# The second expert layer in units of 128 slots, its weights split beforehand in the first attention, and its biases added by VectorE

## The reference

```python
x = x + L0_xattn(ctx, layernorm(x))   # 8 heads of 128, 2113 keys for each batch, 512 queries
x = x + L0_ffn(layernorm(x))          # 8 experts, top 2, fixed capacity of 512
x = x + L1_xattn(ctx, layernorm(x))   # 8 heads of 32, the context asks
x = x + L1_ffn(layernorm(x))          # 8 experts, top 2, as below

def L1_ffn(xf):                       # T = 2048 tokens, D = 256, H = 1024, E = 8
    logits = xf @ Wr + br
    masked = where(logits >= second_largest(logits), logits, -inf)
    weights = softmax(masked)
    h = gelu(xf @ W1[e] + b1[e])      # exact gelu, for every expert e
    out = sum_e weights[:, e] * (h @ W2[e] + b2[e])
```

## Time and profile before

| | |
|---|---|
| time, three runs | 2556.87, 2563.03, 2564.49 us; median 2563.03 |
| profiled execution | 2561.1 us, its span 2559.4 us |
| busy share of the span | PE 89%, DVE 75%, ACT 74%, POOL 71% |
| second expert layer | from 2206 to the end of the span |
| mean granted TensorE clock | 0.967 of full speed |

### The profile page before, as it was taken

The page is one execution under the profiler, slowest core; times in us unless marked ns, Lnnn a source line. Parts: engine busy times, 40 slices in busy tenths (PEclk is TensorE's granted clock), DMA queues, the critical chain, the costliest instruction groups (busy, mean ns, idle before and its releaser), DMA issues. The chain is left out here.

```text
span 2559.4 us, 48371 instructions
## 1 busy us (share of the span) xinstructions
PE 2289.2 (89%) x16979; PEld 1395.7 (55%) x16980; DVE 1921.2 (75%) x3499; ACT 1899.9 (74%) x2979; POOL 1818.0 (71%) x1580
## 2 busy tenths in 40 slices
PE   5999999999999999999998589968888888689996
PEld 3454545444454445445554378835555555468775
DVE  7888778887778887878787556558989899666443
ACT  4787887878877878878888556538879789667554
POOL 2687877787777878777778477617878689556653
PEclk9999999999999999999999699989999999679998
DMA  5000000000000000000000375441202020375323
GB/s 151 1 1 1 27 1 1 1 1 1 27 1 1 1 1 1 1 1 1 1 1 1 106 174 146 97 111 32 60 20 61 11 52 2 126 195 127 49 43 64
DMA packets 90974, 108.66 MB, mean 42 GB/s; under 512 B 18866, under 2 KB 80259, under 8 KB 90707
## 3 DMA queue, kind: packets, MB, share of 16 engines
q1 hardware_dynamic: 68500, 80.57, 10.4%
q0 software_dynamic: 21696, 24.98, 6.3%
q10 hardware_dynamic: 544, 0.00, 0.0%
HBM read 68.75 MB, written 25.88 MB: 37 GB/s over the span
## 5 line engine op out<-in xcount | busy, mean ns | idle before, releaser
L432 POOL TENSOR_TENSOR a_acc<-a_acc,a_pf 128x512 f32<-128x512 f32 (+1 forms) x480 | 679.7, 1416 | 279.9 <-ACT a_pf L601 258.2
L906 DVE TENSOR_TENSOR a_pl<-a_pf,a_ph 128x512 f16<-128x512 f32 x448 | 470.7, 1060 | 23.5 <-ACT a_ph L607 23.5
L2218 POOL TENSOR_TENSOR c_pl<-c_pf,c_ph 128x512 f16<-128x512 f32 x320 | 377.0, 1207 | 118.1 <-ACT c_ph L2315 117.7
L601 ACT ACTIVATE a_pf<-a_psS 128x1024 f32<-128x1024 f32 (+1 forms) x288 | 280.8, 975 | 108.7 <-PE a_psS L624 102.5
L882 DVE TENSOR_REDUCE a_mx<-a_psA 128x1 f32<-128x512 f32 x504 | 330.7, 681 | 26.9 <-PE a_psA L681 25.4
L607 ACT ACTIVATE a_ph<-a_psS 128x1024 f16<-128x1024 f32 (+1 forms) x288 | 281.1, 976 | 0.0
L553 ACT ACTIVATE a_psS<-a_mb 128x1024 f32<-128x1024 f32 x255 | 248.7, 975 | 5.0
L1314 DVE TENSOR_TENSOR f_xn<-f_xn 128x256 f16<-128x256 f32 x312 | 129.6, 424 | 153.2 <-ACT f_xn L1283 126.1
L2551 DVE TENSOR_REDUCE c_wf<-c_psA 128x1 f32<-128x512 f32 x384 | 239.7, 679 | 6.3 <-PE c_psA L2387 5.2
L2308 ACT ACTIVATE c_pf<-c_psS 128x1024 f32<-128x1024 f32 x192 | 201.6, 1050 | 50.6 <-PE c_psS L2416 46.0
L1468 POOL DMA_INDIRECT f_sums<-f_xn,f_sidx x78 | 141.6, 1815 | 135.0 <-DVE f_xn L1867 108.4
(11 more groups left out here) (365 smaller groups left out, 6357.2 us busy)
## 6 DMA issues: line engine op xcount, KB each, us to landing
f_stage<-in_L_ffn_w SPq DMA_DIRECT2D x16, 1024.0 KB
f_stage<-in_L_ffn_W SPq DMA_DIRECT2D x16, 1024.0 KB
c_kst<-c_khs SPq DMA_DIRECT2D x64, 100.1 KB, 2.2
a_cx<-in_ctx SPq DMA_DIRECT2D x4, 1536.0 KB
c_cx<-in_ctx SPq DMA_DIRECT2D x12, 512.0 KB, 3.8
f_sums<-X SPq DMA_DIRECT2D x2, 2048.0 KB, 13.4
f_xrow<-f_xn SPq DMA_DIRECT2D x8, 512.0 KB, 4.8
c_kst<-c_kls SPq DMA_DIRECT2D x32, 100.1 KB, 2.2
```

Of the source, the lines that this page charges most:

```text
L432: g.tensor_tensor(acc[0:k, p, :], acc[0:k, p, :], pf[0:k, q % RF, i, :], ALU.add).then_inc(s_acc, 1)
L601: act.activation(pf[0:r, q % RF, 0:k, :], psS[q % 2][0:r, 0:k, :], ACT.Exp, scale=SCALE).then_inc(s_pF, 1)
L906: v.tensor_tensor(pl[0:r, q % RP, i, :], pf[0:r, q % RF, i, :], ph[0:r, q % RP, i, :], ALU.subtract).then_inc(s_pL, 1)
L2218: g.tensor_tensor(pl[0:r, q % RP, i, :], pf[0:r, q % RF, i, :], ph[0:r, q % RP, i, :], ALU.subtract).then_inc(s_pG, 1)
```

## The change

1. **Units.** In the second expert layer each chunk of 256 slots is made of two units of 128 slots, each with an expert of its own. The table has one number for a unit (HI = 40 entries), padding goes to a multiple of 128, and the number of chunks is 20: half of 32 + 7 units, rounded up. `pe_hidden` does 2 units x 2 parts x 3 matmuls of 128 columns; `pe_output` has the same six matmuls of 256 columns, whose weights now come from two experts. `expert_of` and DVE's `chunk_experts` load two numbers a chunk, and b1 and gates are fetched by unit. PE loads the first numbers before its first `pe_turn`.
2. **Weights.** They are split in the first attention, in 32 pieces of 128x1024 weights, four for each expert (`PIECE_AT`): 19 stand behind unit 3 of a head, 13 behind unit 6. SP loads 512 KB into `tmp`, ACT makes the high half (L599) after the `fill` at the end of unit u, DVE the low half (L966) at the end of unit u + 1, and SP stores both to DRAM (`f1_split`). The second expert layer loads 2 MB of split weights for each expert straight into `w16`; the staging and both split operations are gone there.
3. **Biases.** ACT's gelu has no bias; DVE adds b1, scaled by WS, to the PSUM bank (`dve_add`, L1371, 128x256) and ACT waits for that. The addition for f + 1 stands before the low half of f. `take` of chunk n - 1 stands behind the low half of f = 0 of chunk n.

```diff
+    PIECE_AT = [(n, u) for n in range(NH - 1) for u in (3, 6)
+                if (n < NH - H0 and (n % H0 in (0, 6, 7) or (n % H0 == 1 and u == 3)))
+                or (n >= NH - H0 and (u == 3 or n < NH - H0 + 4))]
...
+            def piece(i):
+                e, second, j = piece_of(i)
+                if i:
+                    sp.wait_ge(s_plo, i)
...
+                    sp.dma_start(wpf, io["L1_ffn_W1"][e, j * P:(j + 1) * P, :]).then_inc(s_pld, 16)
+                sp.wait_ge(s_plo, i + 1)
+                sp.dma_start(wsp[e, :, 2 * second:2 * second + 2, j * 1024:(j + 1) * 1024], wps).then_inc(s_wsp, 16)
...
+            def piece_hi(i):
+                act.wait_ge(s_pld, 16 * i + 16)
+                if i:
+                    act.wait_ge(s_wsp, 16 * i)
+                act.activation(wps[:, 0, :], wpf, ACT.Copy, scale=WS).then_inc(s_phi, 1)
...
+            def piece_lo(i):
+                v.wait_ge(s_phi, i + 1)
+                v.scalar_tensor_tensor(wps[:, 1, :], wpf, WS, wps[:, 0, :], ALU.mult, ALU.subtract).then_inc(s_plo, 1)
...
-    NC = E * CAP // CH if layer == 0 else 2 * T // CH + E - 1
+    NC = E * CAP // CH if layer == 0 else -(-(2 * T // P + E - 1) // IT)
...
-            ps = psH[hidden_slot(L, n, f)][:, 0:CH]
-            for k in range(KC):
-                ks = slice(k * F + f * P, k * F + (f + 1) * P)
-                a, b_ = (w16[:, bass.ds(e, 1), part, ks].rearrange("p a f -> p (a f)") for part in (0, 1))
-                pe.matmul(ps, a, xh[:, p, k, :], start=(k == 0), stop=False)
-                pe.matmul(ps, a, xl[:, p, k, :], start=False, stop=False)
-                ins = pe.matmul(ps, b_, xh[:, p, k, :], start=False, stop=(k == KC - 1))
+            wide = CH // len(es)
+            for u, e in enumerate(es):
+                cs = slice(u * wide, (u + 1) * wide)
+                ps = psH[hidden_slot(L, n, f)][:, cs]
+                for k in range(KC):
+                    ks = slice(k * F + f * P, k * F + (f + 1) * P)
+                    a, b_ = (w16[:, bass.ds(e, 1), part, ks].rearrange("p a f -> p (a f)") for part in (0, 1))
+                    pe.matmul(ps, a, xh[:, p, k, cs], start=(k == 0), stop=False)
+                    pe.matmul(ps, a, xl[:, p, k, cs], start=False, stop=False)
+                    ins = pe.matmul(ps, b_, xh[:, p, k, cs], start=False, stop=(k == KC - 1))
...
-            return pe.value_load(table[0:1, n:n + 1], min_val=0, max_val=E - 1)
+            return tuple(pe.value_load(table[0:1, n * IT + u:n * IT + u + 1], min_val=0, max_val=E - 1)
+                         for u in range(IT))
...
-                bs = b1e[:, p, f:f + 1] if layer else 0.0
+                bs = b1e[:, p, 0, f:f + 1] if layer and not added else 0.0
-                act.wait_ge(L.hP, n * FT + f + 1)
+                act.wait_ge(L.hB if added else L.hP, n * FT + f + 1)
...
+        def dve_add(v, L, n, f):
+            ps = psH[hidden_slot(L, n, f)][:, 0:CH].rearrange("p (u t) -> p u t", t=P)
+            v.wait_ge(L.b1, n + 1)
+            v.wait_ge(L.hP, n * FT + f + 1)
+            v.tensor_tensor(ps, ps, b1e[:, n % 2, :, f:f + 1].broadcast_to([P, IT, P]), ALU.add).then_inc(L.hB, 1)
...
+                if added and not (last and f == FT - 1):
+                    dve_add(v, L, n + (f + 1) // FT, (f + 1) % FT)
...
+                if added and f == 0 and n >= 1:
+                    v.wait_ge(L.hU, done(FT, n - 1, FT - 1))
+                    take_before(n - 1)
...
+            def load_split(e):
+                sp.dma_start(w16[:, e, :, :], wsp[e]).then_inc(s_w[e % 2], 16)
```

More of the change, by code:

```diff
@@ L372, in _ @@
                 load_rows(b)
[L373 to L376 removed]
+            def piece(i):
+                e, second, j = piece_of(i)
+                if i:
+                    sp.wait_ge(s_plo, i)
+                sp.wait_ge(s_xl, sum(1 for w in TORD if IDX[w] < IDX[("M", PIECE_AT[i][0] + 1, 0, 0)]))
+                if second:
+                    sp.dma_start(wpf.rearrange("p (f d) -> p f d", d=D),
+                                 io["L1_ffn_W2"][e].rearrange("(f p) d -> p f d", p=P)[:, 4 * j:4 * j + 4, :]
+                                 ).then_inc(s_pld, 16)
+                else:
+                    sp.dma_start(wpf, io["L1_ffn_W1"][e, j * P:(j + 1) * P, :]).then_inc(s_pld, 16)
+                sp.wait_ge(s_plo, i + 1)
+                sp.dma_start(wsp[e, :, 2 * second:2 * second + 2, j * 1024:(j + 1) * 1024], wps).then_inc(s_wsp, 16)
+            context = 1
+            for i, (n, _) in enumerate(PIECE_AT):
+                while context < B and (context - 2) * H0 + H0 - 3 < n:
+                    sp.wait_ge(s_it, IDX[("T", context - 1, 9)] + 1)
+                    load_context(context)
+                    context += 1
+                piece(i)
         @block.gpsimd
@@ L969, in attention0, with experts @@
     return used
-def experts(nc, X, identf, io, layer, yd, out, pool_sems, small, cleared, load_early=None, early_stats=None):
+def experts(nc, X, identf, io, layer, yd, out, pool_sems, small, cleared, load_early=None, early_stats=None, split=None):
     E, F = 8, 1024
@@ L1149, in __init__ @@
                 self.hP = sem(name + "hP")
+                self.hB = sem(name + "hB") if layer and name == "m" else None
                 self.hH = sem(name + "hH")
@@ L1235, in pe_chunk @@
                 pe.wait_ge(L.xL, n + 3)
-            if splits and layer:
-                pe.wait_ge(s_wl, (n + 3) * PIECES)
+            if layer and L is main and not last:
+                pe.wait_ge(s_wl, e_next[-1] + 1)
             elif splits and p == 1:
@@ L1271, in act_chunk @@
             n = m * 2 + p
-            if layer:
+            added = layer and L is main
+            if layer and not added:
                 act.wait_ge(L.b1, n + 1)
@@ L1320, in dve_chunk @@
                     split_low(v, e, q)
-            v.wait_ge(L.hU, done(FT, n, FT - 1))
-            take(n)
-        LOOPS = ((0, (E - 2) // 2, True), ((E - 2) // 2, PAIRS, False)) if layer else ((0, PAIRS, True),)
+            if not added or last:
+                v.wait_ge(L.hU, done(FT, n, FT - 1))
+                take(n)
+        LOOPS = ((0, PAIRS, not layer),)
         TAIL = range(2 * PAIRS, NC)
@@ L1348, in load_weights @@
                 sp.dma_start(dst, src).then_inc(s_w[half], 16)
-            for half in range(2):
-                load_weights(0, half)
+            def load_split(e):
+                sp.dma_start(w16[:, e, :, :], wsp[e]).then_inc(s_w[e % 2], 16)
+            if layer:
+                sp.wait_ge(s_wsp, 16 * 4 * E)
+                load_split(0)
+            else:
+                for half in range(2):
+                    load_weights(0, half)
             sp.dma_start(yd[0:T, :].rearrange("(t p) c -> p t c", p=P), X[:, :, :]).then_inc(s_base, 16)
@@ L1364, in _ @@
                 sp.dma_start(wrow[T:T + CH, :].rearrange("(t p) e -> p t e", p=P), wst[:, 0:IT, :]).then_inc(s_wd, 16)
-            for half in range(2):
-                load_weights(1, half)
-            with sp.Fori(2, E) as e:
+            if layer:
+                load_split(1)
+                for e in range(E):
+                    sp.wait_ge(s_w[e % 2], 16 * (e // 2 + 1))
+                    sp.sem_inc(s_wl, 1)
+                    if e + 2 == E - 1:
+                        sp.wait_ge(s_bst, 16 * NQ)
+                    if e + 2 < E:
+                        load_split(e + 2)
+            else:
                 for half in range(2):
-                    load_weights(e, half)
+                    load_weights(1, half)
+                with sp.Fori(2, E) as e:
+                    for half in range(2):
+                        load_weights(e, half)
             if load_early:
@@ L1551, in _ @@
             act_turn(act, main, 0, 0)
-            if layer:
-                for q in range(PH, PIECES):
-                    split_high(act, 1, q)
             for first_m, last_m, splits in LOOPS:
@@ L1811, in _ @@
                 v.tensor_scalar(wst[:, :, :], sc[:, :, :], 1.0 / WS, None, ALU.mult).then_inc(s_wst, 1)
-            if layer:
-                for q in range(PH):
-                    split_low(v, 0, q)
             v.wait_ge(s_rk, 1)
@@ L1858, in _ @@
                 v.sem_inc(s_tab, 1)
-                for q in range(PH):
-                    split_low(v, 1, q)
             def take_rows(m, p):
```

154 lines of the change are left out of this document (92 added, 62 removed).

## The result

The changed kernel takes 2630.46 us (median of 4 runs, 2629.3 to 2630.88) against 2563.76 us before (4 runs in the same comparison): ratio 1.0267, 95% interval 1.0255 to 1.0279. It is slower by 67 us, outside the predicted range; the direction was right, the size not. The profiled execution took 2630.55 us, its span is 2628.8 us.

The account below looks back on a forecast made before the run. PE was taken to bound the kernel, its address queue setting the changed second expert layer's pace. Profiled 2561.1 + 22 (pieces) - 4.2 (layer) = 2578.9 us; the median lies 1.9 higher, so 2580, range 2552 to 2602.

Parts of the forecast that it names:

- PE's queue becomes the bound: Second expert layer: twelve address instructions at 0.125 us take 1.50 us a step, passing the array's 1.30; 12.0 us a chunk.
- first rival: Second expert layer: the queue isn't the bound, a chunk stays at 12.2 us, kernel 2547 us; chance 0.12.
- the fourth: Second expert layer: 128-column matmuls aren't half of 256, weight loads paid in full, chunk 16.4 us, kernel 2625 us; chance 0.04.
- Its size: Second expert layer's chunk: 12.0 + 1.3 + 0.44 + 0.3 = 14.0 us, bounds 13.4 and 14.6.
- Two loads: Second expert layer: two table loads stand bare in PE's queue, +1.3 us a chunk.
- PE's queue stands some 0.3 us a chunk: Second expert layer: DVE's preparation delays the low half that output needs, so PE waits 0.3 us a chunk (0 to 0.9).
- The layer's ends: Second expert layer: prelude -2.8 us (bounds -4.5 and 0), after the last turn +4.0 us (+2 to +5).
- The pieces: First attention: 19 pieces behind unit 3 at 1.1 us and 13 behind unit 6 at 0.1, +22 us (+6 to +38).
- third rival: First attention: pieces are dear, 1.65 us behind unit 3 and 0.5 behind unit 6, +38 us, kernel 2597 us; chance 0.14.
- DVE's time was passed on at 0.36: First attention: each us of added DVE work costs 0.36 us; a piece's 1.8 us gives 0.65 us behind unit 3.
- ACT's part: First attention: ACT's 1.02 us operation delays the next exp by 0.8 us, costing PE 0.4 us a piece (0 to 0.8).
- behind unit 6 0.1: First attention: a piece behind unit 6 costs 0.1 us, at most 0.5, as ACT has 1.20 us free there.

Follow-up runs that it names:

- e9: e1 with the second unit's expert used for both units on PE, so units share addresses and one table load: 2562.14 us.
- e8: Changed kernel with joined gathers and constant expert numbers on PE, without address instructions or table loads: 2551.33 us.
- e1: Changed kernel with one gather bringing rows and routing weights together in the second expert layer, 2 gathers a chunk instead of 4: 2606.64 us.
- e6: Kernel before plus the 32 pieces, results unused, with DVE's part in full and ACT's operation on only 8 columns: 2591.0 us.
- e5: Kernel before plus the 32 pieces, results unused, with ACT's part in full and DVE's operation on only 8 columns: 2587.53 us.
- e10: e1 with a third table load on PE in each chunk, its number unused: 2620.49 us.
- e7: Kernel before with only the joined gathers of rows and routing weights in the second expert layer: 2548.93 us.

## Why the prediction was wrong, point by point

**PE's queue becomes the bound: right.** The pace of 0.125 us for an address came out as read, e9 takes it away and e8 shows that the array would do 11.64 us. The first rival is refuted with it, and so is the fourth: pairs of 128 columns start 0.056 us apart. The Trainium skill, "TensorE: Matmul & The Clock Gate", section "Back-to-back issue gap", gives 81 ns for such a pair; the trace doesn't agree here, and by the measured value the array had room. The prediction's remark that the rows at 65 and 256 columns lie below that rule decides nothing, since the section has no sustained figure for either width.

**Its size: short by 0.8 us.** The queue alone makes 14.5 us (e1), where the sum had 13.7 without the wait. Two loads take 1.4 to 1.5 us and not 1.3, and about one start in seven comes 0.20 us after the last one and not 0.125.

**"PE's queue stands some 0.3 us a chunk": the step that failed in this stage.** The wait is there, at L1272 for DVE's low half as said, but it is 1.5 us (16.03 - 14.54), and its cause isn't DVE's preparation: in e1, which has the same preparation, PE stands 0.0 us there. PE's signal of a finished step reaches DVE 2.2 us late while POOL issues the fifth and sixth indirect transfer in a row. In the kernel before ACT took the signal, and had steps to spare; the change put DVE's addition in front of ACT, at the place of the chunk where DVE has its preparation as well. I had taken before's 1.7 us a chunk beside the twelve-step pace as transposes and ordinary waits, and didn't ask what ACT's idle times of 2 to 3.5 us with finished steps in front of it were. With the queue's 0.8 us the chunk is 2.0 us longer than the 14.0 of the prediction, and 17 x 2.03 us add 34.5 us to its 2580.

**The layer's ends: right.** From the last matmul of the second attention to the third turn the change gains 2.3 us in this pair of traces and 3.5 between the means of all traces with and without it, against 2.8 with the bounds 4.5 and 0; the last chunk costs +4.2, as worked out (+4.0).

**The pieces: the term that was mis-sized,** +40 us for +22, past the third rival's 38. Two rates were wrong. DVE's time was passed on at 0.36, from two whole heads in which part of DVE's extra work lay in idle time; at the end of unit 3 it is 1.0 to 1.4 us for 1.5 to 1.7 (e6), about 0.7. ACT's part was 0.4 to 0.9, DVE's wait for POOL in e5 included, where the prediction had 0.4. And "behind unit 6 0.1" holds for odd heads only. The third rival's reason, that DVE's operation and POOL hold each other up, is borne out on DVE's side: L966 takes 1.2 to 2.2 us for the same work, and its end follows the end of a POOL operation. The Trainium skill, "SBUF — State Buffer", section "SBUF: two separate sides", says that a VectorE operation with two SBUF inputs and a GpSimd operation that reads SBUF shut each other out for a whole instruction; the trace agrees, with 0.44 us of waiting in e5's median. How much of this reached PE no run separates.

In sum: predicted +22 - 4 = +18, measured +41 + 28 = +69. Of the 51 us between them 19 are the pieces and 34.5 the chunk (about 20 the late signal, 1.5 us where 0.3 stood, and 14 the queue), less some 3 that the unchanged stages were shorter in this pair of traces. The steps that failed are the wait in the chunk and the price of a piece. Either would have left the time just inside the range's upper end (2580 + 20 or + 19 against 2602); together they pass it.

**What stays open:** why the fifth and sixth indirect transfer hold PE's signals back, whether the number in a row or in a chunk counts, and whether signals of other engines are held too. The runs show that the number matters, and that what the transfers fetch doesn't; the signal is late at ACT and at DVE alike.

## What to carry to other kernels

Where addresses depend on a register, count them, as one counts matmuls: 0.124 us of queue for each, against the array's time in the same step. Smaller units double them while the array's work stays the same. Count what a new step between a signal and its waiter does to the slack behind the worst signal, not the usual one; an idle time that costs nothing today is the first thing that such a step turns into a bound. Work moved into a stage where PE is 97% busy, as in head 27, isn't hidden by the other engines' idle shares: measure one block of it at the place where it will stand.

## What the runs showed of the hardware

- An address instruction on PE takes 0.124 us of its queue (median distance of two starts in the changed kernel; its own record says 46 ns), a table load 0.7 to 0.8 us (e10).
- Weight load and matmul of 128 columns in float16 start 0.056 us apart.
- While POOL issues six indirect transfers in a row, PE's signals come some 2.2 us late at DVE and up to 3.1 us late at ACT, which stands idle up to 3.5 us; with four in a row (e1, e7) they don't once the weights are split. Joined gathers gave 15 us in the kernel before and 24 in the changed one.
- A DVE operation with two SBUF inputs ends just behind POOL's operation when both run in the first attention: 0.01 to 0.03 us behind it with 8 columns (e5), 1.07 to 1.09 us with 1024 (changed kernel), in 30 of 32 cases each.
